# fc2 with y stationary and tokens down the partitions; column scales as rows; fc1's products on ScalarE, fc2's on VectorE

## The reference, cut to what matters

```python
B, S, H, F, G = 4, 2048, 512, 2048, 128          # M (memory) = 128
xn = layernorm(x)
# attention branch: a linear recurrence over time, decay 0.99
q, k, v = xn @ Wq.T, xn @ Wk.T, xn @ Wv.T
#   r_t = q_t @ M.T ;  M = 0.99 * M + v_t.T @ k_t / b
s = (r @ Wo.T) * sigmoid(gate)
# ffn branch
h = layernorm(xn) * ln_gamma + ln_beta
w1 = (fc1_q - 128) * fc1_scales        # one scale per group of 128 rows and column
y = silu(h @ w1 + fc1_bias)
w2 = (fc2_q - 128) * fc2_scales
z = y @ w2 + fc2_bias
g = silu(xn + 0.5 * z)
out = x + s * g
```

## Time and profile before

| | |
|---|---|
| median of three runs | 1339.03 us |
| the profiled execution, its own time | 1339.37 us |
| its span, first to last instruction | 1337.6 us |
| TensorE (PE) busy | 1225.3 us, 92% |
| VectorE (DVE) busy | 1121.2 us, 84% |
| ScalarE (ACT) busy | 1075.0 us, 80% |
| GpSimd (POOL) busy | 382.0 us, 29% |
| granted TensorE clock, mean | 0.977 |

### The profile page before, as it was taken

How to read it: one execution, slowest core, us unless ns; L and a number is a source line. 1 busy time by engine, 2 the same in 40 slices (tenths; PEclk the granted TensorE clock), 3 DMA queues, 4 the chain that set the end, 5 groups by cost and what they waited for, 6 DMA issues and landing times.

```text
span 1337.6 us, 19050 instructions
## 1 busy us (share of the span) xinstructions
PE 1225.3 (92%) x6144; PEld 633.7 (47%) x6144; DVE 1121.2 (84%) x1894; ACT 1075.0 (80%) x1885; POOL 382.0 (29%) x465
## 2 busy tenths in 40 slices
PE   1279999999999999999999999999999999999994
PEld 0034454545545454554545455454545545454551
DVE  5978798888979888897988889798888979888774
ACT  1349888888888888888888888888888888888885
POOL 4115241321414132141413214141422314142111
PEclk8579999999999999999999999999999999999998
DMA  9201021120302112030211203021120303011011
GB/s 327 54 2 32 1 57 40 32 64 2 93 1 64 32 33 64 5 91 0 65 31 33 64 12 84 1 75 21 33 63 15 82 1 82 14 36 29 18 46 32
DMA packets 38837, 61.21 MB, mean 46 GB/s; under 512 B 9553, under 2 KB 9809, under 8 KB 38737
## 3 DMA queue, kind: packets, MB, share of 16 engines
q1 hardware_dynamic: 38448, 59.87, 17.4%
q10 hardware_dynamic: 288, 0.08, 0.0%
HBM read 43.14 MB, written 16.78 MB: 45 GB/s over the span
## 4 chain that ended last, share of the span: by engine, by line
PE 67%; DVE 19%; issue 6%; ACT 6%; POOL 1%; DMA 1%; SPq 0%; DVEq 0%; ACTq 0%; POOLq 0%
PE blk L421 26%; PE blk L438 22%; PE side L382 9%; DVE blk L630 7%; PE side L406 3%; DVE y_lo L641 3%; ACT blk L525 2%; PE side L370 2%; DVE g_lo L610 2%; DVE y_hi L636 2%; ACT y_full L518 2%; PE side L359 1%; DVE g_rows L605 1%; ACT h_full L484 1%; DVE fin L657 1%
## 5 line engine op out<-in xcount | busy, mean ns | idle before, releaser
L630 DVE TENSOR_SCALAR blk<-blk,ratio 128x512 f32<-128x512 f32 x768 | 572.5, 753 | 177.7 <-PE blk L421 172.9
L525 ACT ACTIVATE blk<-blk,ratio 128x512 f32<-128x512 f32 x960 | 625.7, 667 | 73.5 <-PE blk L438 66.6
L421 PE MATMUL blk<-h_hi,q_sb 128*128 128x512 f16 x1024 | 391.7, 383 | 73.2 <-DVE blk L630 35.9
L421 PE MATMUL blk<-h_lo,q_sb 128*128 128x512 f16 x1024 | 390.4, 381 | 0.0
L438 PE MATMUL blk<-y_hi,w_sb 128*128 128x512 f16 x1024 | 388.9, 380 | 0.0
L438 PE MATMUL blk<-y_lo,w_sb 128*128 128x512 f16 x1024 | 388.6, 380 | 0.0
L518 ACT ACTIVATE y_full<-blk,par,last 128x512 f32<-128x512 f32 x256 | 199.3, 779 | 41.3 <-PE blk L421 41.3
L641 DVE SCALAR_TENSOR_TENSOR y_lo<-y_full,up,y_hi 128x512 f16<-128x512 f32 x256 | 228.3, 892 | 0.1
L938 POOL TENSOR_TENSOR out_sb<-fin,s_rows 128x512 f32<-128x512 f32 x62 | 80.2, 1294 | 446.4 <-ACT fin L537 443.1
L421 PEld LDWEIGHTS blk<-h_hi,q_sb 128*128 128x128 f16 x1024 | 100.3, 98 | 218.7 <-DVE blk L630 102.6
L923 POOL TENSOR_TENSOR h_lo<-h_full,h_hi 128x512 f16<-128x512 f32 x64 | 86.8, 1356 | 388.2 <-DVE h_hi L614 373.9
(11 more groups left out here) (132 smaller groups left out, 1151.2 us busy)
## 6 DMA issues: line engine op xcount, KB each, us to landing
xt<-in_x SPq DMA_DIRECT2D x64, 256.0 KB, 4.8
x_again<-in_x SPq DMA_DIRECT2D x256, 64.0 KB, 1.9
out<-out_sb SPq DMA_DIRECT2D x256, 64.0 KB, 1.7
w_sb<-in_q SPq DMA_DIRECT2D x4, 1024.0 KB, 13.8
zt<-in_q SPq DMA_DIRECT2D x2, 1024.0 KB, 15.4
y_hi<-in_q SPq DMA_DIRECT2D x1, 1024.0 KB, 10.1
y_lo<-in_q SPq DMA_DIRECT2D x1, 1024.0 KB, 12.3
s_rows<-in_wqkv SPq DMA_DIRECT2D x1, 768.0 KB, 7.9
```

What stands on the lines that cost most here:

```text
L421: mm = pe.matmul(blk[J % 2][:], q1_sb[:, g, j // 4, w, j % 4 * P:(j % 4 + 1) * P], a[:, c % 2, g, :], start=(g == 0 and n == 0), stop=(g = ...
L525: act.activation(blk2[hb][:], blk2[hb][:], ACT.Copy, scale=ratio2[:, KC * j + hb:KC * j + hb + 1]).then_inc(blk2_scaled, 1)
L630: dve.tensor_scalar(blk[J % 2][:], blk[J % 2][:], ratio1[:, at:at + 1], None, ALU.mult).then_inc(blk_scaled, 1)
```

## The change

Fc2 has y stationary (a tile of 128 tokens) and w2 moving (512 columns). z stands with tokens down the partitions, one PSUM bank for each tile. The transposes of z, `zt` and `finish` are gone. Fc2's scales now differ along the free dimension, so the ratios are rows: `ratio2` is made once, written to DRAM, and read back broadcast to all partitions as `ratio2_rows` (16 by 512 per partition). VectorE multiplies fc2's banks by such a row (`block2_out`), ScalarE does fc1's `rescale` and `y_high`. GpSimd prepares the residual with the bias (`prepare`), adds z (`add_z`) and, at the start, widens fc2's weights in ScalarE's place. The y ring is 6 deep, s_rows a ring of 5; wide fc1 inputs lie in other buffers, and SyncE waits for fc1's conversion before it loads the second chunk. The copy of q and k is one instruction, that of v another. In the last chunk VectorE does part of the finish of the odd tiles.

```diff
-Y_RING = 8
+Y_RING = 6
+S_RING = 5
-TILE_AT, JOB_AT = (0, 12, 24, 36), (0, 3, 5, 8, 10)
-TURN_AT = (43, 49, 54, 59)
-TURN_Z_AT = (18, 21, 26, 30)
-STATS_AT, MOMENTS_AT, ROWS_AT, NORMALISE_AT = (18, 21, 22, 24), (25, 26), 28, (34, 36, 38, 40)
-FIN_LAG, OUT_LAG = 2, 3
-TURN_LAG, HLOW_LAG, READ_LAG = 2, 3, 1
+TILE_AT, JOB_AT = (1, 13, 25, 37), (0, 4, 6, 8, 11)
+TURN_AT = (49, 52, 55, 58)
+QKV_LAG, QKT_LAG, R_LAG, S_LAG, GHIGH_LAG, HFULL_LAG = 1, 1, 1, 1, 1, (2, 2, 2, 3)
+GATE_AT = (16, 17, 21, 29)
+STATS_AT, MOMENTS_AT, NORMALISE_AT = (0, 1, 2, 3), (5, 6), (33, 34, 37, 40)
+MASK_LAG, MEM_LAG, SPLIT_LAG, YHIGH_LAG, YLOW_LAG = 1, 1, (3, 3, 3, 4), 1, 3
+HLOW_LAG = 5
+PREPARE_AT, ROWS_AT = (0, 3, 15, 18), 7
+ADD_AT, OUT_AT = (13, 14, 17, 20), (18, 22, 26, 30)
...
+            sp.dma_start(b2_half[:], b2.partition_broadcast(P)).then_inc(b2_in, 16)
+            sp.wait_ge(ratio2_made, 1)
+            sp.dma_start(ratio2_dram.rearrange("j (p n) -> p j n", n=KC), ratio2[:].rearrange("p (j n) -> p j n", n=KC)).then_inc(ratio2_stored, 16)
...
+            sp.wait_ge(ratio2_stored, 16)
+            for n in range(4):
+                sp.dma_start(ratio2_rows[:, 4 * n:4 * n + 4, :], ratio2_dram[4 * n:4 * n + 4, :].partition_broadcast(P)
+                             ).then_inc(ratio2_in[n], 16)
+            for n in range(2):
+                sp.wait_ge(q1_done[n], FB // 2)
...
-                if job == "turn_z":
-                    if i == 0:
-                        pe.wait_ge(zt_done, KC * (c + 1))
-                    for hb in range(KC):
-                        mm = pe.transpose(bank[:, hb * P:(hb + 1) * P], zt[:, c % 2, hb, i * P:(i + 1) * P], ident[:])
-                    mm.then_inc(z_turned, 1)
...
-                for n, (part, y) in enumerate(terms):
-                    mm = pe.matmul(blk2[hb][:], w2_sb[:, j, part, hb * P:(hb + 1) * P], y[:, J % Y_RING, :],
+                rows = slice(i * P, (i + 1) * P)
+                terms = [(y_hi, 0), (y_lo, 0)] + ([(y_hi, 1)] if slow else [])
+                for n, (y, part) in enumerate(terms):
+                    mm = pe.matmul(blk2[i][:], y[:, J % Y_RING, rows], w2_sb[:, j, part, :],
...
             for G in range(SLOTS):
+                if at := fc1_step(G):
+                    if at[1] < KC - 1:
+                        rescale(*at)
+                    else:
+                        silu(at[0])
+                if (at := fc1_step(G - YHIGH_LAG) if G >= YHIGH_LAG else None) and at[1] == KC - 1:
+                    y_high(at[0])
+                if at := job_behind(G, QKV_LAG, "qkv"):
+                    qkv_copy(*at, side[JOB_BANK[G - QKV_LAG]])
+                if at := job_behind(G, QKT_LAG, "qkt"):
+                    qkt_copy(*at, side[JOB_BANK[G - QKT_LAG]])
+                if at := job_behind(G, R_LAG, "read"):
+                    r_copy(*at, side[JOB_BANK[G - R_LAG]])
+                if at := job_behind(G, S_LAG, "wo"):
+                    s_copy(*at, side[JOB_BANK[G - S_LAG]])
+                if at := job_behind(G, GHIGH_LAG, "turn"):
+                    g_high(*at, side[JOB_BANK[G - GHIGH_LAG]])
+                for k in range(KC):
+                    at = job_behind(G, HFULL_LAG[k], "turn")
+                    if at and at[1] == k:
+                        h_whole(*at, side[JOB_BANK[G - HFULL_LAG[k]]])
+                if at := finishing(G, GATE_AT):
+                    gate_silu(*at)
...
+            def block2_out(J, i):
+                c, j = divmod(J, FB)
+                dve.wait_ge(blk2_done, NT * J + i + 1)
+                if c == 0 and i == 0 and j % 4 == 0:
+                    dve.wait_ge(ratio2_in[j // 4], 16)
+                if j < FB - 1:
+                    dve.tensor_tensor(blk2[i][:], blk2[i][:], ratio2_rows[:, j, :], ALU.mult).then_inc(blk2_scaled, 1)
+                else:
+                    wait(dve, out_free[i], 64 * c)
+                    dve.scalar_tensor_tensor(z_rows[:, i, :], blk2[i][:], unit2[:, 0:1], ratio2_rows[:, j, :],
+                                             ALU.mult, ALU.mult).then_inc(z_out, 1)
...
             for G in range(SLOTS):
                 c, e = divmod(G, STEPS)
                 ahead = c < NCH - 1
+                if at := fc2_step(G):
+                    block2_out(*at)
+                if at := job_behind(G, MASK_LAG, "scores"):
+                    mask_scores(*at, side[JOB_BANK[G - MASK_LAG]])
+                for k in range(KC):
+                    at = job_behind(G, SPLIT_LAG[k], "turn")
+                    if at and at[1] == k:
+                        g_low(*at, side[JOB_BANK[G - SPLIT_LAG[k]]])
+                        h_high(*at)
+                if at := job_behind(G, MEM_LAG, "read"):
+                    remember(*at, side[JOB_BANK[G - MEM_LAG]])
+                if (at := fc1_step(G - YLOW_LAG) if G >= YLOW_LAG else None) and at[1] == KC - 1:
                     y_low(at[0])
...
+            def q2_widen(n):
+                if n == 0:
+                    pool.wait_ge(q2_scaled, 1)
+                    for odd in range(2):
+                        pool.wait_ge(q1_done[odd], FB // 2)
+                if n % 4 == 0:
+                    pool.wait_ge(q2_in[n // 4], 16)
+                wait(pool, q2_done, n - 1)
+                pool.tensor_scalar(wide[:, n % 2, :], q2_in_sb[:, n, :], -ZERO_POINT, up_q2, ALU.add, ALU.mult
+                                   ).then_inc(q2_wide, 1)
...
+                pool.tensor_scalar(xz[:, i % 2, :], x_again[:, i, :], rs[:, c % 3, i:i + 1], nmr[:, c % 3, i:i + 1],
+                                   ALU.mult, ALU.add).then_inc(xz_scaled, 1)
+                pool.wait_ge(xz_scaled, n + 1)
+                pool.tensor_tensor(xz[:, i % 2, :], xz[:, i % 2, :], b2_half[:], ALU.add).then_inc(xz_done, 1)
+
+            def add_z(c, i):
+                pool.wait_ge(xz_done, NT * c + i + 1)
+                pool.wait_ge(z_out, NT * c + i + 1)
+                pool.tensor_tensor(z_rows[:, i, :], z_rows[:, i, :], xz[:, i % 2, :], ALU.add).then_inc(z_sum, 1)
```

More of the change, by code:

```diff
@@ L70, in side_job, with job_behind, finishing @@
         c, e = divmod(G, STEPS)
-        if e not in SIDE:
+        if G < 0 or e not in SIDE:
             return None
         job, i = SIDE[e]
-        c += {"turn": 1, "turn_z": -1}.get(job, 0)
-        return (job, c, i) if 0 <= c < NCH and not (job == "turn" and c == 0) else None
+        c += 1 if job == "turn" else 0
+        return (job, c, i) if c < NCH and not (job == "turn" and c == 0) else None
+    def job_behind(G, lag, kind):
+        at = side_job(G - lag)
+        return at[1:] if at and at[0] == kind else None
+    def finishing(G, at):
+        c, e = divmod(G, STEPS)
+        return (c - 1, at.index(e)) if c > 0 and e in at else None
     def fc1_step(G):
@@ L327, in _ @@
                         load_again(c, i)
-            for n in range(2):
-                sp.wait_ge(out_free[n], 64 * 2 * NCH)
+            for n in range(NT):
+                sp.wait_ge(out_free[n], 64 * NCH)
         @block.tensor
@@ new lines, in h_whole, with qkv_copy @@
+                               bias=beta_s[:, k:k + 1], scale=gamma_s[:, k:k + 1]).then_inc(h_full_done, 1)
+            def qkv_copy(c, i, bank):
+                act.wait_ge(qkv_done, 4 * c + i + 1)
+                act.wait_ge(row_c_done, c + 1)
+                wait(act, read_done, 4 * c + i - 1)
+                act.activation(qkv[:, i % 2, 0:2 * M], bank[:, 0:2 * M], ACT.Copy, scale=row_c[:, c % 2, 0, i:i + 1]
+                               ).then_inc(qkv_out, 1)
+                act.activation(qkv[:, i % 2, 2 * M:], bank[:, 2 * M:3 * M], ACT.Copy,
+                               scale=row_c[:, c % 2, 1, i:i + 1]).then_inc(qkv_out, 1)
@@ new lines, in qkt_copy, with r_copy, s_copy @@
+            def qkt_copy(c, i, bank):
+                act.wait_ge(qkt_done, 4 * c + i + 1)
+                wait(act, read_done, 4 * c + i)
+                act.activation(qk_t[:], bank[:, 0:2 * P], ACT.Copy).then_inc(qkt_out, 1)
+            def r_copy(c, i, bank):
+                act.wait_ge(read_done, 4 * c + i + 1)
+                wait(act, wo_done, 4 * c + i)
+                act.activation(r_t[:], bank[:, 0:P], ACT.Copy).then_inc(r_out, 1)
+            def s_copy(c, i, bank):
+                act.wait_ge(wo_done, 4 * c + i + 1)
+                n = 4 * c + i
+                if c == 0 and i == 0:
+                    act.wait_ge(decay_done, 1)
+                if n < S_RING:
+                    act.wait_ge(wqkv_split, 1)
+                else:
+                    act.wait_ge(z_mul, n - S_RING + 1)
+                act.activation(s_rows[:, n % S_RING, :], bank[:], ACT.Copy, scale=powers[:, 0:1]).then_inc(s_out, 1)
@@ L748, in top_of_q1 @@
                                          apply_absolute_value=True)
+            dve.wait_ge(par_in, 16)
+            top(0, gamma_c)
+            top(1, beta_c)
+            top(2, s1_c)
+            top(3, b1_c)
+            hold(1, s2_c, KC, FB)
```

(11 more changed lines are left out.)

380 lines of the change are left out of this document (154 added, 226 removed).

## The result

| | before | changed |
|---|---|---|
| median of the runs, us | 1338.7 (4 runs) | 1356.6 (4 runs, 1356.2 to 1357.0) |
| ratio, 95% interval | | 1.0131 [1.0114, 1.0149] |
| span of the profiled execution, us | 1337.6 | 1354.4 |
| a chunk in the middle, us | 77.62 | 78.50 |

What follows compares the result with a forecast made beforehand. TensorE was taken to set the pace: floor 72.6 us plus waits for ScalarE and the mask made 76.8 a chunk against 77.6. 1339.4 - 11 - 3.5 - 0.3 - 2, less 0.4, gave 1323 us, range 1298 to 1352.

Steps and rivals of the forecast that it cites:

- The durations: Start to start on VectorE and ScalarE: product by a row 0.60 us, y_high 0.61, rescale 0.58, silu 0.66.
- TensorE's work per chunk: TensorE's floor in a steady chunk once z's transposes, 1.7 us, are removed: 72.6 us.
- The turns: Slots 50 to 63: ScalarE's overfull queue makes TensorE wait 1.5 us a chunk.
- the mask: Wait before read, behind the slot's VectorE product: 0.9 us in the first tile, then 0.27, 0.45 and 0.27.
- In slots 16 to 63: First chunk: ScalarE no longer widens fc2's weights, VectorE has about 59 us to do; 3.5 us less.
- the sum of the steady chunk: A middle chunk: 72.6 + 1.5 + 0.8 + 0.9 + 0.27 + 0.45 + 0.27 = 76.8 us against 77.6.
- Scores: Slots 17 and 29: a gate precedes qkt's copy on ScalarE, so scores waits 0.48 and 0.35, 0.8 us.
- The last chunk: The run's final chunk has no turns and changes by 0.3 us, taken off the time.
- The start: Before fc2's first step: slot 16 stays at 85.75 us, 4 us either way.
- The end: After the last chunk: some 5 us shorter without transposes, 3 longer for fc2's last products; 2 less.
- VectorE is the bound: Rival, chance 0.30: VectorE's queue before the mask sets the pace, 78.4 us a chunk, 1348 us in all.
- Waits unchanged: Rival, chance 0.18: TensorE's waits stay 3.3 us a chunk, giving 75.9 a chunk and 1309 us.

## Why the forecast was wrong, step by step

**Right.** The durations: product by a row 0.59 to 0.60 start to start (709.64 with two in 1.26 us, the second 0.67 long), y_high 0.61, rescale 0.57, silu 0.66. The other price for the product, 0.66 by the Trainium skill, page "VectorE: DVE Perf Modes", section on the TRN2 errata, is not borne out by these 960 products as a distance of starts; their duration, 692 ns, lies above it. TensorE's work per chunk, 72.8 for 72.6. The turns, 1.7 for 1.5, and the mask, 1.55 for 1.9: 0.33 in three tiles for 0.27, 0.45 and 0.27, and 0.56 in the first for 0.9. In slots 16 to 63 the time fell by 4.1 for 3.5 (first fc2 matmul at 90.58, second chunk at 148.62, against 86.56 and 148.67). Y_low's mean was 869 ns, where above 890 had been named as a sign; 16 of them are 2.1 us a chunk above 0.74, for the 5 us that had been put down to GpSimd. Two small sums of the forecast do not come out: 1322.6 less 0.4 is 1322 and not 1323, and 0.70 less a tenth of 0.42 is 0.66 and not 0.61.

**The step that failed first is the sum of the steady chunk**, 76.8 for 78.5: it put every wait outside the turns, two of the scores and the mask at nothing, without a reason. No single term that it has is far off. Scores waits 1.2 instead of 0.8 (0.61 and 0.50 at the two gates for 0.48 and 0.35, and 0.1 in the first tile); the f32 passes that start late add 0.6, of which the forecast knew nothing; small latenesses of 0.05 to 0.22 at fc1's steps add 0.7, and the turns and the work 0.35 together; the mask gives 0.35 back. That is 0.4 + 0.6 + 0.7 + 0.35 - 0.35 = 1.7 us, times 14 is 24 of the 34 us by which the forecast missed. The 1.2 us more of the second chunk, where VectorE's queue has no gap from 145.8 us to the first tile's mask, was not foreseen either. The net gain left, 0.8 a chunk, was smaller than the 1.3 of waits left out. The mask is the largest cost that one edit takes away, but it was in the sum, and slightly too dear.

**The last chunk**: "has no turns and changes by 0.3", taken off; it grew by 1.3. Before, the waits of a chunk lay mostly at the turns, and without them TensorE is only 0.8 us late in the last chunk (two products of 0.37 among it, one of them in the earlier trace rows). In the changed kernel the mask and scores stay, 1.9 and 0.8 by the forecast's own prices, which eats up the 1.7 us of z's transposes and leaves about +0.1 instead of -0.3. Most of the other 1.2 are the waits that the steady chunk's sum lacks too: the f32 passes and fc1's steps make 1.2, scores is 0.4 dearer, the mask 0.6 cheaper.

**The start**: slot 16 was put at 85.75 with 4 us either way. It began at 84.35, inside that, but its fc2 step waited 5.64 us for its weights and came 4.0 later than before, which took the gain behind it. The cause is GpSimd: its next large operation starts 7.17 us after the maximum over partitions, and the halved bias, the row scales and fc2's first weights stand in a row behind it. The experiment that shortened this row shows a further wait close behind, for the mask.

**The end**: "2 less" and it was 2.1 more. The drain at VectorE's pace, from slot 64 to fc2's last matmul, was 0.8 longer for 3 (10.1 for 9.3). After fc2's last matmul 20.7 us remained, where 14.4 had been counted; the two prepares are 4.5 of these 6.

**The rivals.** That VectorE is the bound fails as it was put, as a load of 78 us; the trace shows it busy 63.7 of 78.5. But its place, "the queue before the mask", was right, and the price hung on an order within a slot and not on the load: 1327 with the mask first, 1357 with it second. And for 15 us of the chunk VectorE is in fact nearly full (14.35), and y's high halves filled it. That the measured time lies near this rival's 1348 is chance: its mechanism, a full VectorE, was not at work. "Waits unchanged" (1309) was nearer to what a better order gives, 1314.5.

## What to carry to other kernels

An operation that the pace-setting engine will ask for next stands ahead of bulk work in its queue, even when the bulk work is of the same slot: here one exchange of two calls moved the result from 1.3% slower to 0.9% faster. Work moved between engines is priced by the stretch in which the receiving queue is fullest, not by its mean share, and a gain at one wait can be given back at the next wait of the same engine (half of it with qkt's copy first, none with the mask first), so edits of order are tried together. When a forecast's net gain is smaller than the sum of its priced waits, the waits that nobody priced can decide its sign.

## What was not expected of the hardware

After PARTITION_ALL_REDUCE, shown as 0.38 us, GpSimd's next operation started 7.17 us later in the changed kernel and 7.49 in the run with the earlier bias, with no wait that the profile shows; VectorE had used the result 1.25 us after the recorded end (74.43 for 73.18). The kernel before has such a gap too, 7.01 us behind its first reduction at 48.34. What fills it is open. A pass of two f32 matmuls that starts late, be it by 0.01 us, is followed up to 0.30 us later instead of 0.22, at every scores and read that was late. And z_rows' operations with two inputs in SBUF, on VectorE and GpSimd at once at the end, took 1.63 to 1.75 us on VectorE, where the last, alone, took 0.69.
